# All of lookup level one on GpSimd, and the last layer-norm taken tile by tile on VectorE

## The chip, the cores and the metric

The kernel runs on one core of a Trainium2 chip. The core has four compute engines that run their own instruction streams in order and meet only at semaphores: TensorE (PE in the profile, its weight loads PEld), VectorE (DVE), ScalarE (ACT) and GpSimd (POOL). A fifth stream, SyncE (SP), issues all DMA transfers here. The metric is device microseconds from launch to end; lower is better. A profiled execution lists its own time, its span (first to last recorded instruction) and every instruction.

## What is computed

Two transformer layers over x of shape 4 x 256 x 256 (batch, sequence, width), each with attention, a sum and a layer-norm, a feed-forward part, a sum and a layer-norm:

```python
x = L0_attn_x                                        # (4, 256, 256)
x = layernorm(x + attn0(x))       # 32 query heads of 8, 8 key/value heads
x = layernorm(x + ffn0(x))        # weights rounded to fp8, scaled; inner width 768
x = layernorm(x + attn1(x))       # 16 query heads of 16, 8 key/value heads
x = layernorm(x + ffn1(x))        # w = lut[idx]: 16-entry table, int indices; inner width 688
# attn: softmax(q k^T / sqrt(d)) v, then the output projection
# ffn:  (silu(x @ gate) * (x @ up)) @ down
# layernorm(x) = (x - mean) / sqrt(var + 1e-5) over the width
```

## The kernel before

**Jobs.** There are eight jobs: 0 to 3 are layer 0 for batches 0 to 3, and 4 to 7 are layer 1 for the same batches. A job goes through these steps, whose names are used below. `q`, `kv`: projections on PE, split by ACT and POOL into three bf16 parts, which SP stacks into `QS` and `KS` (`qstack`, `kstack`). `max.j.u`: 4 matmuls into the PSUM tile `MM` and one VectorE reduce of 1024 columns to row maxima (16 units in a layer-0 job, 8 in a layer-1 job, 96 in all; there is one `MM`, so a unit's matmuls wait for the reduce before it). `mt`: the maxima are split, transposed, and put into `QS` by SP. `score`, `pv`: scores, exp on ACT (L838), probabilities times values. `turn`, `back`, `wo`: division, transposes and output projection, then `xadd` (POOL) and a layer-norm, whose statistics are VectorE's (L924, L929) and whose rest is POOL's (L653 to L657). `tr`: transpose of x. `gu.j.i`, `hsplit`, `down`: the feed-forward part in six row blocks; `down` of a job sums in one PSUM bank, ACT copies that out (L808), POOL adds it to x (`dsum`, L701), and the second layer-norm follows. `out`: the result's DMA, one per batch.

**Weights of the feed-forward parts.** Both are made on the core during the layer-0 jobs. Layer 0: 12 chunks (`q8`: ACT casts, a VectorE predicated copy at L1019, `q8w` on POOL). Layer 1: 10 chunks of 432 columns. For chunk c, `lutix` (ACT) makes bytes of the indices, `lutbits` (VectorE) picks out the four bits, and `lut1` computes eight table candidates from bit 0: `LV[:, i] = LT[2i] + bit * LD[i]`. Four of the eight are POOL's (L724, steps `lut1.c.0` and `lut1.c.1`) and four ACT's (L885, `lut1.c.2` and `lut1.c.3`), two instructions a step. `lut2`, `lut3`, `lut4` (VectorE, L1042) are predicated copies of 1728, 864 and 432 columns that leave one value; `lutlow` rounds it (ACT, L892) and takes the rest (POOL, L713), and SP writes that to DRAM. After chunk 9, ten `reload` transfers bring the low parts to SBUF over the space of `LV`. `lut1.c` waits for `lutlow` of chunk c - 1, and `lut2.c` waits for all eight candidates. The layer-1 feed-forward part cannot start before all of this.

**Order.** Nothing is scheduled at run time. `ORDER` holds one list of steps for each engine, written out by hand or by a program outside the kernel; each engine issues its list in order, and a step whose wait isn't met holds up everything behind it on that engine. An `@` in the list of PE names the one of three PSUM banks (`FB`) that the step takes.

Of the kernel before, what the change touches and what calls it, by code (L numbers as in the profile page):

```python
# [81 lines left out]
def unit0(j):  # L82
# [182 lines left out]
def two_layer_kernel(nc, x, xt, wq0, wk0, wv0, wo0, gate0, up0, down0, gs0, us0, ds0,  # L265
# [7 lines left out]
    with ExitStack() as ctx:  # L273
# [456 lines left out]
        def _(act):  # L730
            for step in order("ACT"):
# [144 lines left out]
                elif kind == "lut1":  # L876

                    _, c, part = step
                    if c == 0 and part == 2:
                        act.wait_ge(lut_steps, 1)  # L880
                    act.wait_ge(bit_done, c + 1)
                    if c >= 1:
                        act.wait_ge(low_done, c)
# [422 lines left out]
```

## Time and profile before

| | |
|---|---|
| runs | 363.84, 364.13, 361.82 us (median 363.84) |
| profiled execution | 362.06 us, of which the span 360.2 us |
| PE busy | 299.7 us (83%) |
| DVE busy | 258.1 us (72%) |
| ACT busy | 246.3 us (68%) |
| POOL busy | 195.2 us (54%) |
| `max` reduces, L950 | 96 of 1219 ns, 117.0 us |
| `lut1` on POOL, L724 | 40 of 715 ns, 28.1 us |
| `lut1` on ACT, L885 | 40 of 738 ns, 27.4 us |
| `lut2` to `lut4`, L1042 | 30 of 1419 ns, 42.6 us |

How to read it: the shares are averages over the whole span. The part up to about 200 us holds the four layer-0 jobs' attention and the making of the weights; the part behind it is mostly matmuls. Where a view gives "idle before <-X", the engine stood still until X was done.

### The profile page before, as it was taken

Reading aid. Unit: us, or ns where it says so; the run is one execution under the profiler, and the core shown is the slowest. Engines: PE = TensorE matmul, PEld = TensorE weight load, DVE = VectorE, ACT = ScalarE, POOL = GpSimd, SP = SyncE. Lnnn points to the kernel's source line nnn. Section 1 sums busy time; section 2 is a strip of 40 time slices with the busy share of each in tenths; the row PEclk is TensorE's granted clock in tenths of the full one; section 3 lists DMA queues with packets and bytes.
Section 4 is the critical chain, followed back from the end, with each engine's and each line's share of the span. In section 5 each row is a group of like instructions: output and inputs, shape, how many; then the busy total and the mean of one; then the engine's idle time right before and its main releaser. Section 6 shows DMA issues by size and latency. Waiting matters only on the chain.

```text
span 360.2 us, 7105 instructions
## 1 busy us (share of the span) xinstructions
PE 299.7 (83%) x2608; PEld 198.9 (55%) x2608; DVE 258.1 (72%) x399; ACT 246.3 (68%) x449; POOL 195.2 (54%) x261
## 2 busy tenths in 40 slices
PE   8446127687869897998979999999999999999990
PEld 7334002222426462564535765687778887979990
DVE  7695999898889897999986676656754657416341
ACT  3766677988588868797677776687677636654340
POOL 5756562404195348983398422564664346528763
PEclk9858555879899999999999999999999999999996
DMA  6468571201331000230001650032013000000000
GB/s 196 135 159 208 151 237 29 89 23 51 100 92 48 5 5 25 67 95 0 24 5 39 189 181 4 1 85 52 0 32 105 0 5 31 1 2 31 0 31 29
DMA packets 24872, 23.06 MB, mean 64 GB/s; under 512 B 3542, under 2 KB 24838, under 8 KB 24838
## 3 DMA queue, kind: packets, MB, share of 16 engines
q1 hardware_dynamic: 24838, 22.61, 22.2%
q8 instruction: 21, 0.34, 0.4%
q14 instruction: 13, 0.11, 0.1%
HBM read 10.47 MB, written 3.26 MB: 38 GB/s over the span
## 4 chain that ended last, share of the span: by engine, by line
PE 58%; DVE 13%; POOL 8%; ACT 8%; issue 7%; SPq 4%; DMA 2%; POOLq 0%; DVEq 0%; ACTq 0%
PE FB L1236 16%; PE PV L1179 9%; PE FB L1249 8%; PE MM L1124 6%; DVE LV L1042 5%; DVE MX L950 5%; PE SC L1158 4%; PE FB L1208 3%; PE SC L1153 2%; ACT PB L838 2%; PE FB L1078 2%; PE FB L1191 2%; SPq L542 2%; DMA QS<-QP 2%; ACT LV L885 2%
## 5 line engine op out<-in xcount | busy, mean ns | idle before, releaser
L950 DVE TENSOR_REDUCE MX<-MM 128x4 f32<-128x1024 f32 x96 | 117.0, 1219 | 40.1 <-PE MM L1124 39.5
L838 ACT ACTIVATE PB<-SC 128x1024 f32<-128x1024 f32 x96 | 98.2, 1023 | 31.7 <-PE SC L1153 19.5
L1124 PE MATMUL MM<-KS,QS 62*128 62x256 bf16 (+1 forms) x384 | 47.5, 292 | 33.6 <-DVE MX L950 24.8
L1179 PE MATMUL PV<-PB,VP 128*32 128x256 f32 x768 | 61.8, 408 | 1.3 <-ACT PB L838 1.3
L706 POOL TENSOR_TENSOR HL<-HF,HH 128x256 fp32r<-128x256 f32 (+1 forms) x48 | 37.6, 787 | 45.0 <-ACT HH L815 45.0
L1124 PEld LDWEIGHTS MM<-KS,QS 62*128 62x128 bf16 (+1 forms) x384 | 19.4, 97 | 59.4 <-DVE MX L950 39.4
L1042 DVE COPY_PREDICATED LV<-LB,LV 128x1728 f32<-128x1728 uint8 (+2 forms) x30 | 42.6, 1419 | 3.5 <-POOL LV L724 3.1
L1236 PE MATMUL FB<-XH,W 128*128 128x256 f32 x192 | 42.9, 305 | 0.5 <-DVE HF L1002 0.5
L1236 PE MATMUL FB<-XL,W 128*128 128x256 f32 x192 | 38.5, 282 | 0.0
L999 DVE SCALAR_TENSOR_TENSOR AA<-TH,FB 128x256 f32<-128x256 f32 (+1 forms) x48 | 20.0, 416 | 22.4 <-ACT TH L829 19.6
L1153 PE MATMUL SC<-QS,KS 64*128 64x256 bf16 x256 | 26.5, 287 | 9.8 <-ACT PB L838 7.8
L1236 PEld LDWEIGHTS FB<-XH,W 128*128 128x128 f32 x192 | 30.3, 190 | 6.5 <-issue 3.9
L1236 PEld LDWEIGHTS FB<-XL,W 128*128 128x128 f32 x192 | 29.5, 189 | 0.2 <-POOL XL L679 0.2
L1179 PEld LDWEIGHTS PV<-PB,VP 128*32 128x32 f32 x768 | 16.9, 110 | 22.6 <-issue 15.2
L724 POOL TENSOR_SCALAR LV<-LB,LD,LT 128x432 f32<-128x432 uint8 x40 | 28.1, 715 | 1.6 <-POOL LO L713 0.9
L885 ACT ACTIVATE LV<-LB,LT,LD 128x432 f32<-128x432 uint8 x40 | 27.4, 738 | 2.0 <-POOL LO L713 2.0
L657 POOL TENSOR_SCALAR X<-X,NM,RSTD 128x256 f32<-128x256 f32 x32 | 21.9, 693 | 1.7
L815 ACT ACTIVATE HH<-HF 128x256 fp32r<-128x256 f32 (+1 forms) x48 | 19.6, 412 | 4.6 <-DVE HF L1002 4.3
L1153 PEld LDWEIGHTS SC<-QS,KS 64*128 64x128 bf16 x256 | 8.9, 98 | 24.5 <-ACT PB L838 14.3
L1249 PE MATMUL FB<-W,HH 128*128 128x256 f32 (+1 forms) x96 | 22.0, 311 | 0.0
L664 POOL TENSOR_SCALAR W<-TH 128x384 fp32r<-128x384 f32 x12 | 6.9, 574 | 27.8 <-DVE TH L1019 27.8
L924 DVE BATCH_NORM_STATS2 BST<-X 128x6 f32<-128x256 f32 x32 | 11.9, 415 | 12.2 <-POOL X L701 11.9
(96 smaller groups left out, 578.5 us busy)
## 6 DMA issues: line engine op xcount, KB each, us to landing
QS<-QP SPq DMA_DIRECT2D x48, 128.0 KB, 2.4
IX<-in_idx SPq DMA_DIRECT2D x10, 216.0 KB, 4.0
dw<-LO SPq DMA_DIRECT2D x10, 216.0 KB, 2.1
W1L<-dw SPq DMA_DIRECT2D x10, 216.0 KB, 3.8
KS<-KP SPq DMA_DIRECT2D x24, 64.0 KB, 2.0
XT<-in_xt SPq DMA_DIRECT2D x4, 256.0 KB, 3.0
X<-in_x SPq DMA_DIRECT2D x4, 256.0 KB, 4.0
out<-X SPq DMA_DIRECT2D x4, 256.0 KB, 2.1
```

What stands on the lines that cost most here:

```text
L657: ins = pool.tensor_scalar(X[:, batch(j), t, :], X[:, batch(j), t, :], NM[:, n % 2, t:t + 1], RSTD[:, n % 2, t:t + 1], ALU.add, ALU.mult)
L706: pool.tensor_tensor(HL[0:r, i, :], HF[0:r, c % 2, :], HH[0:r, i, :].bitcast(F32), ALU.subtract).then_inc(h_parts, 1)
L724: ins = pool.tensor_scalar(LV[:, i, :], LB[:, 0, :], LD[:, i:i + 1], LT[:, 2 * i:2 * i + 1], ALU.mult, ALU.add)
L838: act.activation(PB[:, quad % PB_QUADS, kt, :, :], SC[:, :, :], ACT.Exp, scale=DH[layer(j)] ** -0.5).then_inc(exp_done, 1)
L885: ins = act.activation(LV[:, i, :], LB[:, 0, :], ACT.Identity, scale=LD[:, i:i + 1], bias=LT[:, 2 * i:2 * i + 1])
L950: dve.tensor_reduce(mx, MM[:, :, :].rearrange("p (f i) s -> p f i s", f=2), axis=AX.X, op=ALU.max).then_inc(max_red, 1)
L1042: ins = dve.copy_predicated(LV[:, 0:LUT // 2:2 * gap, :], mask, LV[:, gap:LUT // 2:2 * gap, :])
L1124: ins = pe.matmul(MM[:, 2 * f + i, :], QS[lo:lo + r, j % NST, qs + h, qt * P:(qt + 1) * P], keys(j)[lo:lo + r, j % NST, ks, :], start=True ...
L1153: ins = pe.matmul(SC[:, place(j, c), :], keys(j)[lo:lo + r, j % NST, ks, kt * P:(kt + 1) * P], QS[lo:lo + r, j % NST, qs + u % 4, :], star ...
L1179: ins = pe.matmul(PV[32 * c:32 * c + 32, r % 2, :], v, PB[:, quad % PB_QUADS, kt, place(j, c), :], start=part == 0, stop=part == (3, 1)[la ...
L1236: ins = pe.matmul(bank[:, w * S:(w + 1) * S], ffn_up(l, w, t, i)[part], xs[:, t, :], start=k == 0, stop=k == len(products) - 1)
L1249: ins = pe.matmul(bank[:, t * D:(t + 1) * D], hs[0:rows(l, i), i, t * P:(t + 1) * P], ffn_down(l, i)[part], start=i + k + t == 0, stop=(i, ...
```

## The change

Three things. `lut1` is four steps of POOL's list and none of ACT's; L742 of the new kernel is the POOL instruction that was L724 before, now 80 times. The last job's `down` goes to the two banks of `MM`, one row tile after the other; VectorE adds each tile to x straight from PSUM and takes its statistics and `var + eps`, POOL does one power per tile, VectorE the final subtract and multiply, and SP sends each tile by itself. All five lists are new.

```diff
 # waits of lut2 (VectorE)
-                        dve.wait_ge(level1, 2 * (c + 1))
-                        dve.wait_ge(level1_act, 2 * (c + 1))
+                        dve.wait_ge(level1, 4 * (c + 1))
 # ScalarE
-                elif kind == "lut1":
...
-                    for i in range(2 * part, 2 * part + 2):
-                        ins = act.activation(LV[:, i, :], LB[:, 0, :], ACT.Identity, scale=LD[:, i:i + 1],
-                                             bias=LT[:, 2 * i:2 * i + 1])
-                    ins.then_inc(level1_act, 1)
 # TensorE, down of the last job
+                    if j == JOBS - 1:
+                        if i == 0:
+                            pe.wait_ge(max_red, unit0(JOBS))
+                        for t in range(TT):
+                            for k, (part, hs) in enumerate(products):
+                                ins = pe.matmul(MM[:, 2 * t, :], hs[0:rows(l, i), i, t * P:(t + 1) * P],
+                                                ffn_down(l, i)[part], start=i + k == 0,
+                                                stop=(i, k) == (5, len(products) - 1))
+                            if i == 5:
+                                ins.then_inc(down_half, 1)
+                        continue
 # VectorE, down and fin of the last job
+                    for t in range(TT):
+                        dve.wait_ge(down_half, t + 1)
+                        link(dve.tensor_tensor(X[:, b, t, :], X[:, b, t, :], MM[:, 2 * t, :], ALU.add))
+                        link(dve.bn_stats(BST[:, n % 2, t, :], X[:, b, t, :]))
+                        link(dve.bn_aggr(MV[:, n % 2, t, :], BST[:, n % 2, t, :]))
+                        dve.tensor_scalar(VE[:, n % 2, t:t + 1], MV[:, n % 2, t, 1:2], 1.0, EPS, ALU.mult,
+                                          ALU.add).then_inc(var_last, 1)
+                elif kind == "fin":
...
+                    for t in range(TT):
+                        dve.wait_ge(rstd_last, t + 1)
+                        dve.tensor_scalar(X[:, b, t, :], X[:, b, t, :], MV[:, n % 2, t, 0:1], RSTD[:, n % 2, t:t + 1],
+                                          ALU.subtract, ALU.mult).then_inc(x_last, 1)
 # GpSimd, last job
+                            pool.wait_ge(var_last, t + 1)
+                            pool.tensor_tensor(RSTD[:, n % 2, t:t + 1], VE[:, n % 2, t:t + 1], NHALF[:, 0:1],
+                                               ALU.pow).then_inc(rstd_last, 1)
 # SyncE, last job
+                            sp.wait_ge(x_last, t + 1)
+                            sp.dma_start(out[batch(j), t * P:(t + 1) * P, :], X[:, batch(j), t, :]).then_inc(out_wr, 16)
 # the lists, one line of five tables
-        "q.0.0@0 q.0.1 kv.0.0@1 kv.0.1 kv.1.0@2 kv.1.1 q.1.0@0 q.1.1 max.0.0 q.2.0@1 q.2.1 q.3.0@0 q.3.1 max.0.1 "
+        "q.0.0@0 q.0.1 kv.0.0@1 kv.0.1 kv.1.0@2 kv.1.1 q.1.0@0 q.1.1 max.0.0 q.2.0@1 q.2.1 max.0.1 q.3.0@0 q.3.1 "
```

**Start of the program, PE.** Before, the second unit of maxima (`MM`) stands behind 8 matmuls of `q` for jobs 2 and 3 (two `FB` fills), and the third behind `kv.2`:

```order
L1124 MATMUL MM<-KS,QS 128x256 x4
L1078 MATMUL FB<-XT,WQ 128x256 x8
L1124 MATMUL MM<-KS,QS 128x256 x4
L1098 MATMUL FB<-XT,WK 64x256 x2
L1103 MATMUL FB<-WV,XT 128x64 x4
```

Now:

```order
L1150 MATMUL MM<-KS,QS 128x256 x4
L1104 MATMUL FB<-XT,WQ 128x256 x4
L1150 MATMUL MM<-KS,QS 128x256 x4
L1104 MATMUL FB<-XT,WQ 128x256 x4
L1124 MATMUL FB<-XT,WK 64x256 x2
L1150 MATMUL MM<-KS,QS 128x256 x4
L1129 MATMUL FB<-WV,XT 128x64 x4
```

The second unit moved ahead of `q.3`, the third ahead of half of `kv.2`.

**The same place, POOL.** Before, between the casts `q8w.0` (`W`) and the split of q of job 1 (`QR`), four candidates of chunk 0 (`LV`):

```order
L724 TENSOR_SCALAR LV<-LB,LD,LT 128x432 x2
L664 TENSOR_SCALAR W<-TH 128x384
L724 TENSOR_SCALAR LV<-LB,LD,LT 128x432 x2
L669 TENSOR_TENSOR QR<-QR,QP 128x512
L664 TENSOR_SCALAR W<-TH 128x384
```

Now eight, six of them ahead of that split and of `q8w.1`:

```order
L742 TENSOR_SCALAR LV<-LB,LD,LT 128x432 x2
L680 TENSOR_SCALAR W<-TH 128x384
L742 TENSOR_SCALAR LV<-LB,LD,LT 128x432 x6
L685 TENSOR_TENSOR QR<-QR,QP 128x512
L680 TENSOR_SCALAR W<-TH 128x384
```

Every chunk looks like this, with two to six candidates in a row. Chunk by chunk VectorE's `lut2` comes later in its list: `lut2.5`, behind `max.1.14` before, is now behind `max.2.4`; `lut2.7` went from behind `max.2.13` to behind `max.3.1`. For chunk 9 all three copies (`lut2.9`, `lut3.9`, `lut4.9`) stood ahead of `max.4.0` and now stand behind `gu.2.1`, `gu.2.5` and `max.4.5`. Up to `max.4.0` VectorE's new list lacks these three copies and is otherwise a reordering. PE's list up to `max.4.0` lacks `kv.5` and half of `q.5` (`q.5.1`) and has `score.3.7` and `pv.3.1.1` instead.

**The end, VectorE.** Before, the last rows (`AA` and `HF` are the last block of `gu`):

```order
L1002 SCALAR_TENSOR_TENSOR HF<-FB,AA 48x256
L924 BN_STATS BST<-X 128x6 x2
L929 BN_AGGR MV<-BST 128x2 x2
```

Now:

```order
L1029 SCALAR_TENSOR_TENSOR HF<-FB,AA 48x256
L1004 TENSOR_TENSOR X<-X,MM 128x256
L1005 BN_STATS BST<-X 128x6
L1006 BN_AGGR MV<-BST 128x2
L1007 TENSOR_SCALAR VE<-MV 128x1
L1004 TENSOR_TENSOR X<-X,MM 128x256
L1005 BN_STATS BST<-X 128x6
L1006 BN_AGGR MV<-BST 128x2
L1007 TENSOR_SCALAR VE<-MV 128x1
L1015 TENSOR_SCALAR X<-X,MV,RSTD 128x256 x2
```

The sum and the last multiply came over from POOL, and ACT's copy is gone.

## Rows read from the trace of the kernel before

**Rows 1.** Busy time per stretch; columns: length, then busy (x count) by engine.

```profile
30.00:60.00 30.00, 11.06 (x87) 3.89 (x86) 27.28 (x29) 21.18 (x44) 14.38 (x18) 0.60 0.55 163
60.00:100.00 40.00, 31.61 (x296) 12.02 (x288) 34.58 (x44) 33.12 (x57) 12.41 (x18) 0.83 0.21 62
100.00:200.00 100.00, 86.72 (x859) 49.59 (x856) 87.24 (x119) 79.29 (x133) 67.93 (x80) 1.00 0.14 39
200.00:347.00 147.00, 146.61 (x1265) 114.14 (x1265) 85.13 (x175) 93.08 (x176) 75.73 (x109) 1.00 0.15 44
```

**Rows 2.** Waits of PE from 0 to 200 us: total, times, longest.

```profile
PE MM L1124 <- DVE MX L950: 24.6, 23, 5.3
...
PE SC L1153 <- ACT PB L838: 7.8, 13, 0.9
```

**Rows 3.** Timeline of PE around the second unit: start, length.

```profile
23.45 6.61 PE L1078 MATMUL FB<-XT,WQ 128*128 128x256 f32 x16 [1.20 <-DMA XT<-in_xt]
29.99 0.39 PE L1124 MATMUL MM<-KS,QS 62*128 62x256 bf16 x4
```

**Rows 4.** Timeline of VectorE in the same stretch.

```profile
18.18 2.08 DVE L1042 COPY_PREDICATED LV<-LB,LV 128x1728 f32<-128x1728 uint8 x1 [3.12 <-POOL LV L724]
...
30.42 1.22 DVE L950 TENSOR_REDUCE MX<-MM 128x4 f32<-128x1024 f32 x1 [2.92 <-PE MM L1124]
```

**Rows 5.** The costliest groups: busy, mean ns, idle before.

```profile
L1042 DVE COPY_PREDICATED LV<-LB,LV 128x1728 f32<-128x1728 uint8 (+2 forms) x30 | 42.6, 1419 | 3.5 <-POOL LV L724 3.1
...
L999 DVE SCALAR_TENSOR_TENSOR AA<-TH,FB 128x256 f32<-128x256 f32 (+1 forms) x48 | 20.0, 416 | 22.4 <-ACT TH L829 19.6
...
L724 POOL TENSOR_SCALAR LV<-LB,LD,LT 128x432 f32<-128x432 uint8 x40 | 28.1, 715 | 1.6 <-POOL LO L713 0.9
L885 ACT ACTIVATE LV<-LB,LT,LD 128x432 f32<-128x432 uint8 x40 | 27.4, 738 | 2.0 <-POOL LO L713 2.0
```

**Rows 6.** Timeline of POOL at one `lut1`, of VectorE's `mt` beside it and alone.

```profile
48.45 2.76 POOL L724 TENSOR_SCALAR LV<-LB,LD,LT 128x432 f32<-128x432 uint8 x4
...
49.91 0.65 DVE L964 SCALAR_TENSOR_TENSOR MS<-MX,MS 128x32 bf16<-128x32 f32 x1
...
68.65 0.19 DVE L964 SCALAR_TENSOR_TENSOR MS<-MX,MS 128x32 bf16<-128x32 f32 x1
```

**Rows 7.** Timeline of VectorE: `lut2.9`, and the reduce of `max.4.0`.

```profile
187.81 2.10 DVE L1042 COPY_PREDICATED LV<-LB,LV 128x1728 f32<-128x1728 uint8 x1
...
197.34 1.23 DVE L950 TENSOR_REDUCE MX<-MM 128x4 f32<-128x1024 f32 x1 [2.35 <-PE MM L1124]
```

**Rows 8.** Timeline of PE: `kv.5` (two rows) and `q.5`.

```profile
189.89 1.13 PE L1098 MATMUL FB<-XT,WK 128*128 128x256 f32 x4
190.86 1.05 PE L1103 MATMUL FB<-WV,XT 128*128 128x128 f32 x8
...
194.36 2.00 PE L1078 MATMUL FB<-XT,WQ 128*128 128x256 f32 x8
```

**Rows 9.** Chain that ended last: start, length, what; its last matmuls.

```profile
347.56 4.47 PE FB L1249 x36
```

**Rows 10.** Timeline of all engines behind the last matmul.

```profile
352.06 0.60 ACT L808 ACTIVATE RAW<-FB 128x512 f32<-128x512 f32 x1 [2.55 <-PE FB L1249]
...
354.03 0.75 DVE L924 BATCH_NORM_STATS2 BST<-X 128x6 f32<-128x256 f32 x2 [4.97 <-POOL X L701]
354.82 0.25 DVE L929 BATCH_NORM_AGGREGATE MV<-BST 128x2 f32<-128x6 f32 x2
...
355.70 0.71 POOL L655 TENSOR_TENSOR RSTD<-VE,NHALF 128x2 f32<-128x2 f32 x1
356.51 1.10 POOL L657 TENSOR_SCALAR X<-X,NM,RSTD 128x256 f32<-128x256 f32 x2
...
357.64 0.37 SPq L610 DMA_DIRECT2D out<-X  x1
```

**Rows 11.** DMA issues of the output: KB each, median us to landing.

```profile
out<-X SPq DMA_DIRECT2D x4, 256.0 KB, 2.1
```

More of the change, by code:

```diff
@@ L412, in two_layer_kernel @@
         x_new = sem("x_new")
+        x_last = sem("x_last")
+        var_last = sem("var_last")
+        rstd_last = sem("rstd_last")
+        down_half = sem("down_half")
         th_done = sem("th_done")
@@ L429, in two_layer_kernel @@
         level1 = sem("level1")
-        level1_act = sem("level1_act")
         lut_done = sem("lut_done")
@@ L611, in _ @@
                                  X[:, batch(j), :, :]).then_inc(out_wr, 16)
-            sp.wait_ge(out_wr, 16 * B)
+            sp.wait_ge(out_wr, 16 * (B + TT - 1))
         @block.gpsimd
@@ L651, in _ @@
                     n = norms[step]
+                    if step == ("down", JOBS - 1):
+                        for t in range(TT):
+                            pool.wait_ge(var_last, t + 1)
+                            pool.tensor_tensor(RSTD[:, n % 2, t:t + 1], VE[:, n % 2, t:t + 1], NHALF[:, 0:1],
+                                               ALU.pow).then_inc(rstd_last, 1)
+                        continue
                     pool.wait_ge(mv_done, n + 1)
@@ L692, in _ @@
                     j = step[1]
+                    if j == JOBS - 1:
+                        continue
                     b = batch(j)
@@ L804, in _ @@
                     j = step[1]
+                    if j == JOBS - 1:
+                        continue
                     act.wait_ge(down_ready, j + 1)
@@ L875, in _ @@
                     act.activation(IB[:, :], IX[:, c % 2, :], ACT.Copy).then_inc(ib_done, 1)
-                elif kind == "lut1":
[L878 to L883, printed above, removed]
-                    for i in range(2 * part, 2 * part + 2):
-                        ins = act.activation(LV[:, i, :], LB[:, 0, :], ACT.Identity, scale=LD[:, i:i + 1],
-                                             bias=LT[:, 2 * i:2 * i + 1])
-                    ins.then_inc(level1_act, 1)
                 elif kind == "lutlow":
@@ L987, in _ @@
                     b = batch(j)
-                    dve.wait_ge(x_sum, j + 1)
-                    layer_norm(b, step)
+                    if j < JOBS - 1:
+                        dve.wait_ge(x_sum, j + 1)
+                        layer_norm(b, step)
+                        continue
+                    n = norms[step]
+                    dve.wait_ge(x_new, n - 1)
+                    for t in range(TT):
[6 more added lines that the diff above has]
+                elif kind == "fin":
+                    b = batch(JOBS - 1)
+                    n = norms["down", JOBS - 1]
+                    for t in range(TT):
+                        dve.wait_ge(rstd_last, t + 1)
+                        dve.tensor_scalar(X[:, b, t, :], X[:, b, t, :], MV[:, n % 2, t, 0:1], RSTD[:, n % 2, t:t + 1],
+                                          ALU.subtract, ALU.mult).then_inc(x_last, 1)
                 elif kind == "gu":
@@ L1246, in _ @@
                     products = ((0, HH), (0, HL), (1, HH))[:2 + l]
+                    if j == JOBS - 1:
+                        if i == 0:
+                            pe.wait_ge(max_red, unit0(JOBS))
+                        for t in range(TT):
+                            for k, (part, hs) in enumerate(products):
[4 more added lines that the diff above has]
+                                ins.then_inc(down_half, 1)
+                        continue
                     for k, (part, hs) in enumerate(products):
```

237 rows, old and new, of the table ORDER are left out of this document.

## Prediction, made before the changed kernel ran

> **What bounds the kernel now.** I read the stretches first [rows 1]. From 200 to 347 us PE is busy 146.6 of 147 us: nothing there can be gained except by giving PE less work or letting it begin earlier. From 30 to 200 us PE is not full: it is busy 11.1 of 30, 31.6 of 40 and 86.7 of 100 us. In the same three stretches VectorE is busy 27.3, 34.6 and 87.2 us, the highest or nearly the highest load of any engine. The waits of PE say the same [rows 2]: 24.6 us in 23 waits of a `max` unit for the reduce before it, and only 7.8 us in 13 waits of a `score` for ACT's exp. So up to about 200 us VectorE's list sets the pace, with PE's list order deciding how well it is fed; behind that PE does. The crossing is the reduce of `max.4.0` at 197.34 us [rows 7]. The kernel ends with a serial tail: the last matmul ends just before ACT's copy at 352.06 us, and copy, sum, statistics, power, multiply and one transfer follow, each waiting for the one before it [rows 10, 11].
>
> Hence the questions: does the new order bring `max.4.0` sooner, how much PE work stands behind it, and what is left of the tail. All sums are against the profiled execution (362.06 us).
>
> **The tail.** Before, from 352.06 to the end of POOL's multiply at 356.51 + 1.10 = 357.61 us: 5.55 us, then the transfer [rows 10]. After, PE finishes row tile 0 three matmuls before the end. The 36 matmuls of `down` take 4.47 us [rows 9], 0.124 us each, so 0.37 us early, at about 351.7 us. Per tile VectorE then has an add from PSUM, 0.42 us like the 256-column form of L999 [rows 5], half of 0.75 us of statistics, half of 0.25 us of aggregation and a one-column operation of 0.1 us [rows 10]: 1.0 us, and with three own-semaphore waits of about 0.1 us each 1.3 us. Two tiles: 351.7 + 2.6 = 354.3 us. The power of tile 1 costs 0.71 us plus a crossing of 0.1 us, 355.1 us; the last subtract and multiply 0.35 to 0.55 us (POOL took 0.55 for a tile), 355.5 us. Against 357.61 us this is 2.1 us less; the transfer is half as large, but its 2.1 us to landing [rows 11] is kept since four transfers of one size don't show how it depends on size. Ends: 1.3 us if every link costs 0.2 us and the multiply 0.55, 2.8 us if the half transfer lands sooner. **-2.1 us.**
>
> **The start.** The second unit of maxima waits in PE's list behind 6.61 us of projections [rows 3], and VectorE stands still 2.92 us before its reduce at 30.42 us [rows 4]. The new list puts only half of those projections ahead of it: it can begin about 3.3 us sooner. Against this stands `lut1.0`: eight candidates on POOL cost 8 x 0.715 = 5.7 us instead of 2.9 us on each of two engines [rows 5], so `lut2.0`, which began at 18.18 us as soon as POOL was done [rows 4], begins 2.8 us later, and the first reduces queue behind it. Part of that is free, since VectorE has the 2.9 us hole behind it and the next cast is put ahead. Walking the new list by these durations brings the first `mt` about 3.3 us sooner with 0.8 us of copies fewer ahead of it. I take **-2.0 us**, ends 0 and -3.3.
>
> **Chunk 9 goes behind the crossing.** VectorE's list up to `max.4.0` lacks `lut2.9`, `lut3.9`, `lut4.9`. Ten chunks are 42.6 us [rows 5], with stalls in it; the first copy of chunk 9 took 2.10 us [rows 7] and the other two are a half and a quarter of its columns, together 3.9 us. They land where VectorE is busy 85 of 147 us [rows 1], and `reload` still has some 40 us until job 4's feed-forward part. Cover gone, that is if a unit of maxima had to wait for them there, they would cost up to the same 3.9 us again. **-3.9 us**, ends 0 and -4.3.
>
> **More PE work behind the crossing.** `kv.5` is 1.13 + 1.05 us and half of `q.5` is 1.0 us [rows 8], less overlap of 0.2: 3.0 us that are now behind `max.4.0`. Ahead of it instead are a `score` of four matmuls, priced as the four of a `max` (0.39 us, [rows 3]), and a `pv` part, again four matmuls of 256 columns, 0.4 to 0.65 us. As PE is full from there on, the difference counts: **+2.0 us**, ends +1 and +2.5.
>
> **`lut1` alone on POOL.** In sum POOL gets 28.6 us, and from 100 to 200 us, where five of the ten chunks lie, it goes from 67.9 busy to about 82 of 100 us [rows 1]. POOL does not become full, but `lut2.c` now waits 2.8 us more for its candidates, and behind it on VectorE stand units of maxima and behind these PE. The new list gives room for this: between `lutbits.c` and `lut2.c` VectorE has mostly four to six units of maxima, six to nine us. POOL's list between them holds 5.7 us of candidates and, for chunk 5, a layer-norm of some 2.8 us too (8.5 against 7.6 us), for chunk 7 the layer-norm of `down.0` ahead and one `hsplit` between. I price two or three late chunks at 0.5 to 1 us: **+1.5 us**, ends 0 and +6.
>
> **Port contention.** While POOL ran `lut1`, VectorE's small `mt` operation took 0.65 us, against 0.19 us with POOL still [rows 6]. `lut1.c` cannot meet the copies of its own chunk, since they wait for it; it can meet the 12 casts' predicated copies, `mt` and `lutbits`. Some 40 such operations, a sixth of them beside a new `lut1`, at up to 0.46 us each is 3 us at the most, and part of it in VectorE's idle time. **+1.0 us**, ends 0 and +3. The Trainium skill (SBUF — State Buffer, "Who interferes with whom") calls the shared port pair of VectorE and GpSimd an exclusive lock, held for a whole instruction, so that the loser "fully blocks". By that rule an operation that starts in a random place in a 0.71 us instruction loses 0.36 us on the mean, and the forty would add 2.4 us instead of 1.0; the trace's 0.46 us agrees with it.
>
> **ACT relieved.** It loses 40 x 0.738 us = 29.5 us of instructions (27.4 us busy, as they overlap) [rows 5]. ACT was busy 33.1 of 40 us from 60 to 100 us and 79.3 of 100 behind that [rows 1], but PE waited for exp only 7.8 us [rows 2], and much of that hides under the next reduce. **-1.0 us**, ends 0 and -5.
>
> **Sum.** -2.1 - 2.0 - 3.9 + 2.0 + 1.5 + 1.0 - 1.0 = -4.5 us: 357.6 us on the scale of the profiled execution. That execution lies 1.8 us below the median of the runs; on the median's scale it is 359.3. I put the forecast between them, at **358.5 us**.
>
> **The rivals.** (a) *Only the tail counts.* The lists trade places without gain: what the start and chunk 9 save goes into the later `kv.5`, later copies and waits for `lut2`. For it: the terms of the lists sum to only -2.4 us, and in-order lists lose easily what they gain. Against it: the 2.92 us hole and chunk 9's copies are real and their new places are free. 363 (between the profiled execution and the median) - 2.1 gives 361 us. Chance 0.27. (b) *Slower: the candidates come late in nearly every chunk.* The place is VectorE's wait at `lut2.c`; each chunk late by the 2.8 us that POOL's extra four candidates take costs up to 10 x 2.8 = 28 us, of which the room in the list takes most. It decides against the change where the mean lateness is above 0.6 us (6.0 us with the 1.5 already counted cancel the gain), and at 1.4 us, half of the extra, the time is 358.5 + 14 - 1.5 = 371 us. For it: VectorE's list is served in order and is the bound there, POOL is at 82%, and POOL's durations stretch where it meets VectorE's copies. Against it: six to nine us of room. Chance 0.10. (c) *ACT was the hidden limit.* With ACT free, exp follows its score at once and `mt`, `stage` and casts come sooner; the 7.8 us of waits mostly go and the start gives its full 3.3 us: 358.5 - 4 - 1.3 = about 353.5 us. For it: ACT's 83% from 60 to 100 us. Against it: these waits are short (0.9 us at most). Chance 0.18. (d) *The tail does not do what it says:* the four linked operations per tile cost as much as the shorter chain saves. 360.5 us; it would need 0.4 us more per link. Chance 0.03. My forecast keeps 0.42.
>
> **Range and chances.** 353 us leaves out the better half of what is beyond (c), 363 us takes in (a) and (d) whole; (b) lies outside. About 1% either way is what a measurement of this kernel can tell from no change: faster means under 360.2 us, slower above 367.5 us. Faster: my forecast nearly whole (0.39), (c) (0.18) and a little of (a) and (d) (0.05), 0.62. Slower: (b) without its mild end, 0.09. Same: 0.29.
>
> **What would show it.** In the new profile: the second reduce of `MX` at about 27 us instead of 30.4; `max.4.0` (the 65th of 96 reduces) at 191 to 194 us instead of 197.3; no wait of VectorE's copies for POOL over 1 us behind the first chunk; PE full from there on; from the last matmul to the last multiply 3.5 us instead of 5.6, and two transfers in the place of one. Wrong would be: waits of L1068 for L742 of several us in total (rival b); `max.4.0` sooner but the last matmul not (PE's later work or new waits behind 200 us took it); or PE's waits for exp gone and the crossing below 190 us (rival c).

## The result, and the profile after

The changed kernel takes **358.64 us** (median, 357.35 to 358.93) beside 363.05 us (361.82 to 364.13) for the kernel before on the same chip: ratio 0.988, interval 0.9855 to 0.991. The forecast was 358.5 us, inside 353 to 363. The sum came out; several of its terms did not, as the experiments show, so part of the hit is luck.

The profiled execution of the changed kernel took 358.93 us, 357.0 us of it span. First the stretches, with the columns of [rows 1]:

```profile
30.00:60.00 30.00, 12.41 (x91) 4.51 (x94) 27.57 (x30) 15.83 (x34) 23.99 (x30) 0.58 0.57 160
60.00:100.00 40.00, 30.50 (x328) 11.46 (x320) 36.32 (x45) 32.86 (x55) 20.89 (x27) 0.97 0.23 64
100.00:200.00 100.00, 85.61 (x824) 48.88 (x826) 88.34 (x119) 66.05 (x107) 73.92 (x97) 0.98 0.12 35
200.00:347.00 147.00, 146.55 (x1258) 114.23 (x1255) 88.11 (x177) 94.88 (x180) 79.74 (x114) 1.00 0.16 46
```

PE is as full from 200 us on as before. ACT lost 13 us between 100 and 200 us, POOL gained 6 us there. The column behind the five engines is the clock granted to TensorE, as a share of the higher of its two levels (1.00 is 2.4 GHz, 0.50 is 1.2 GHz, values between are a mixture in time). From 60 to 100 us it is 0.97, where it was 0.83 [rows 1]. No run changes the clock by itself, so what this is worth stays open; PE's busy time for its 2608 matmuls is 298.9 us beside 299.7, which leaves little for it.

VectorE was to get no new work but the short tail, and yet is busier in every stretch. The page says where (the busy line, then three of the costliest groups):

```profile
PE 298.9 (84%) x2608; PEld 197.6 (55%) x2608; DVE 267.7 (75%) x405; ACT 224.6 (63%) x408; POOL 222.9 (62%) x297
...
L958 DVE TENSOR_REDUCE MX<-MM 128x4 f32<-128x1024 f32 x96 | 117.1, 1220 | 34.9 <-PE MM L1150 34.1
...
L742 POOL TENSOR_SCALAR LV<-LB,LD,LT 128x432 f32<-128x432 uint8 x80 | 56.3, 716 | 0.9 <-DVE LB L1054 0.6
...
L1068 DVE COPY_PREDICATED LV<-LB,LV 128x1728 f32<-128x1728 uint8 (+2 forms) x30 | 45.9, 1531 | 3.0 <-POOL LV L742 2.8
```

VectorE's total went from 258.1 to 267.7 us; 1.9 us of the growth are the six instructions that the new tail adds. The thirty copies have the same count as in [rows 5], and their mean went from 1419 to 1531 ns. They wait for POOL 2.8 us in all, nearly all of it at the first chunk (3.1 us before): candidates that come late are not the matter.

The start, on VectorE, answers to [rows 4], and the maxima's crossing to [rows 7]:

```profile
22.23 3.04 DVE L1068 COPY_PREDICATED LV<-LB,LV 128x1728 f32<-128x1728 uint8 x1 [2.63 <-POOL LV L742]
25.31 1.23 DVE L958 TENSOR_REDUCE MX<-MM 128x4 f32<-128x1024 f32 x1
...
28.60 1.21 DVE L958 TENSOR_REDUCE MX<-MM 128x4 f32<-128x1024 f32 x1
...
192.20 1.22 DVE L958 TENSOR_REDUCE MX<-MM 128x4 f32<-128x1024 f32 x1 [1.88 <-PE MM L1150]
193.46 0.51 DVE L970 TENSOR_SCALAR MS<-MX 128x32 bf16<-128x32 f32 x1
194.00 0.65 DVE L972 SCALAR_TENSOR_TENSOR MS<-MX,MS 128x32 bf16<-128x32 f32 x1
194.64 1.23 DVE L958 TENSOR_REDUCE MX<-MM 128x4 f32<-128x1024 f32 x1
197.62 1.23 DVE L958 TENSOR_REDUCE MX<-MM 128x4 f32<-128x1024 f32 x1 [1.76 <-PE MM L1150]
```

The first reduce is 3.0 us later than before (22.28 us), the second 1.8 us sooner, and the unit of `max.4.0` begins at 194.64 instead of 197.34 us. The starts of a few steps on VectorE, read from the timelines in list order, show when the new order is ahead (for a unit of maxima the start of its reduce; the last two columns are experiments described below):

| start of, us | before | after | tail alone | lists and POOL alone |
|---|---|---|---|---|
| `max.0.0` | 22.28 | 25.31 | 21.97 | 24.58 |
| `mt.0.0` | 49.40 | 48.96 | 48.94 | 48.38 |
| `mt.0.1` | 68.44 | 65.30 | 67.98 | 64.76 |
| `max.2.0` | 110.03 | 103.05 | 109.31 | 102.84 |
| `mt.2.1` | 153.97 | 149.75 | 153.25 | 150.29 |
| `mt.3.1` | 194.25 | 193.46 | 193.55 | 193.25 |
| `max.4.0` | 197.34 | 194.64 | 196.63 | 194.43 |
| `max.5.0` | 221.40 | 220.15 | 220.68 | 219.95 |
| `lut2.5` | 105.28 | 114.24 | 104.54 | 114.03 |
| `lut2.9` | 187.81 | 201.97 | 187.11 | 201.77 |
| end of the last matmul | 352.03 | 351.44 | 351.25 | 351.33 |

The lead is 7.0 us at `max.2.0`. In part that is because the copies of each chunk from the sixth on come some 9 to 14 us later, and the lead shrinks as they follow. At `mt.3.1` 0.8 us are left and at the last matmul 0.6 us.

The tail, all engines from the last matmul on, answers to [rows 10]; the last row is the page's kind for the output, to be read against [rows 11]:

```profile
351.16 0.28 PE L1279 MATMUL MM<-W1L,HH 48*128 48x256 f32 x1
351.19 0.42 DVE L1004 TENSOR_TENSOR X<-X,MM 128x256 f32<-128x256 f32 x1 [2.71 <-PE MM L1279]
...
352.40 0.41 DVE L1004 TENSOR_TENSOR X<-X,MM 128x256 f32<-128x256 f32 x1
...
353.60 0.40 DVE L1015 TENSOR_SCALAR X<-X,MV,RSTD 128x256 f32<-128x256 f32 x1
353.76 0.65 POOL L665 TENSOR_TENSOR RSTD<-VE,NHALF 128x1 f32<-128x1 f32 x1 [0.64 <-DVE VE L1007]
354.03 1.20 SPq L616 DMA_DIRECT2D out<-X  x2
354.44 0.41 DVE L1015 TENSOR_SCALAR X<-X,MV,RSTD 128x256 f32<-128x256 f32 x1 [0.45 <-POOL RSTD L665]
```

```profile
out<-X SPq DMA_DIRECT2D x2, 128.0 KB, 1.7
```

From the end of the last matmul (351.44) to the end of the last multiply (354.85) it is 3.4 us instead of 5.55, and a half transfer lands in 1.7 us instead of 2.1.

### The profile page after: what moved, and what is told of

Same layout as the page of the kernel before. It is cut to its first block, busy times and chain, and to the rows that moved or that the text cites. A ratio compares the mean times of both kernels' runs of the same rounds, so it can differ in the third digit from the quotient of the medians.

```text
span 357.0 us, 7099 instructions
## 1 busy us (share of the span) xinstructions
PE 298.9 (84%) x2608; PEld 197.6 (55%) x2608; DVE 267.7 (75%) x405; ACT 224.6 (63%) x408; POOL 222.9 (62%) x297
## 4 chain that ended last, share of the span: by engine, by line
PE 55%; DVE 16%; POOL 9%; ACT 6%; issue 6%; SPq 5%; DMA 2%; POOLq 0%; ACTq 0%; DVEq 0%
PE FB L1262 14%; PE PV L1205 9%; PE FB L1287 7%; DVE LV L1068 6%; PE MM L1150 5%; DVE MX L958 5%; PE SC L1184 4%; PE FB L1234 4%; POOL LV L742 4%; ACT PB L858 3%; PE SC L1179 3%; PE FB L1217 2%; SPq L546 2%; POOL LO L731 2%; PE FB L1243 2%
## 5 line engine op out<-in xcount | busy, mean ns | idle before, releaser
L1150 PE MATMUL MM<-KS,QS 62*128 62x256 bf16 (+1 forms) x384 | 47.6, 293 | 35.4 <-DVE MX L958 27.3
L1205 PE MATMUL PV<-PB,VP 128*32 128x256 f32 x768 | 60.4, 400 | 2.9 <-ACT PB L858 2.6
L724 POOL TENSOR_TENSOR HL<-HF,HH 128x256 fp32r<-128x256 f32 (+1 forms) x48 | 37.1, 777 | 32.2 <-ACT HH L835 32.1
L742 POOL TENSOR_SCALAR LV<-LB,LD,LT 128x432 f32<-128x432 uint8 x80 | 56.3, 716 | 0.9 <-DVE LB L1054 0.6
L1068 DVE COPY_PREDICATED LV<-LB,LV 128x1728 f32<-128x1728 uint8 (+2 forms) x30 | 45.9, 1531 | 3.0 <-POOL LV L742 2.8
L731 POOL TENSOR_TENSOR LO<-LV,W 128x432 f32<-128x432 f32 x10 | 11.5, 1145 | 21.7 <-ACT W L900 21.6
L706 POOL TENSOR_TENSOR X<-X,WF 128x512 f32<-128x512 f32 x8 | 11.2, 1395 | 16.5 <-ACT WF L820 16.5
L1104 PE MATMUL FB<-XT,WQ 128*128 128x256 f32 x64 | 18.8, 440 | 1.2 <-DMA XT<-in_xt 1.2
L1184 PE MATMUL SC<-QS,KS 98*128 98x512 bf16 x64 | 19.2, 382 | 0.4 <-ACT PB L858 0.4
L1287 PE MATMUL FB<-W,HH 128*128 128x256 f32 (+1 forms) x84 | 19.1, 309 | 0.2 <-POOL HL L724 0.2
```

Source lines behind the costliest of these rows:

```text
L724: pool.tensor_tensor(HL[0:r, i, :], HF[0:r, c % 2, :], HH[0:r, i, :].bitcast(F32), ALU.subtract).then_inc(h_parts, 1)
L742: ins = pool.tensor_scalar(LV[:, i, :], LB[:, 0, :], LD[:, i:i + 1], LT[:, 2 * i:2 * i + 1], ALU.mult, ALU.add)
L1068: ins = dve.copy_predicated(LV[:, 0:LUT // 2:2 * gap, :], mask, LV[:, gap:LUT // 2:2 * gap, :])
L1150: ins = pe.matmul(MM[:, 2 * f + i, :], QS[lo:lo + r, j % NST, qs + h, qt * P:(qt + 1) * P], keys(j)[lo:lo + r, j % NST, ks, :], start=True ...
L1184: ins = pe.matmul(SC[:, 2 * f:2 * f + 2, :], keys(j)[lo:lo + r, j % NST, ks, kt * P:(kt + 1) * P], QS[lo:lo + r, j % NST, qs:qs + 2, :], s ...
L1205: ins = pe.matmul(PV[32 * c:32 * c + 32, r % 2, :], v, PB[:, quad % PB_QUADS, kt, place(j, c), :], start=part == 0, stop=part == (3, 1)[la ...
```

## The experiments

All twelve were timed in five rounds beside the kernel before, with four to twelve runs each. "Ratio" is to that kernel in the same rounds, with its 95% interval. The median of the kernel before moved between 361.72 and 363.05 us from one set of rounds to another, so kernels of different sets are compared by their ratios.

**Taking the change apart.** `t1_tail`: the kernel before, its lists and its shared level one, with the new tail. `t2_lists`: the new lists and all of level one on GpSimd, with the old tail.

> The kernel before with the new tail only: its five lists and ScalarE's half of level one stay, the last job's sums go tile by tile on VectorE from the two maxima banks. By the two traces, the time from the last matmul to the end of the span went from 352.03 -> 360.2 us (8.2 us) to 351.44 -> 357.0 us (5.6 us), so this kernel should be 2.6 us faster than before (about 360.4 us against 363.05 us); my forecast's own term was 2.1 us. Rival: the tail gains only because the new lists leave VectorE and GpSimd idle there; then it is under 1 us faster. Last matmul in the trace: unmoved at about 352 us by both.

> The five new lists and GpSimd alone on level one, with the old tail (copy by ScalarE, sum and layer-norm by GpSimd, one transfer). Theory A: the lists move the last matmul by only 0.6 us (352.03 to 351.44 us in the traces), because what chunk 9's deferral and the start gain is lost to the port shared by VectorE and GpSimd and to the projections put off; this kernel is then 0.5 to 2 us faster than before (361 to 362.5 us). Rival: the lists carry most of the whole 4.4 us gain, which the single traces understate; then it is 3 us or more faster (under 360 us).

The tail alone: 359.76 us, ratio 0.9939 (0.9915 to 0.9962), 2.2 us. The lists and GpSimd alone: 361.31 us, ratio 0.9974 (0.9955 to 0.9992), 0.9 us. Together 3.2 us by the ratios, and the whole change measured 0.988, which is 4.3 us: they add up within the intervals. The tail is between half (2.2 of 4.3) and two thirds (2.2 of 3.2) of the gain.

The profiled executions do not show the rest. Set beside the tail alone, the changed kernel has its first reduce 3.3 us later, then needs 5.3 us less from there to `max.4.0`, and 2.2 us more from `max.4.0` to the end of the last matmul (156.80 against 154.62 us), which ends 0.2 us later. The profiled execution of `t1_tail` took 358.60 us, near the lowest of its twelve runs (358.46 to 361.55), so a gain of 1 to 2 us is seen only in the ratios.

**Everything on GpSimd under the old lists** (`t4_pool`), and **the new lists with ACT sharing again** (`t3_share`: four of the eight candidates go back to ACT, at places in its list that I chose by the times in the trace).

```diff
 t4_pool, list of GpSimd, every chunk
-lut1.c.0 .. lut1.c.1
+lut1.c.0 .. lut1.c.1 lut1.c.2 lut1.c.3
```

> The kernel before, lists and tail as they were, but each chunk's four ScalarE candidates stand behind GpSimd's four. Nothing in the lists gives room for them. Theory A: VectorE's copies wait 1 to 2.8 us more in many of the ten chunks and its operations grow beside GpSimd's longer runs, the end is 3 to 9 us later, 366 to 372 us. Rival B: ScalarE's relief pays for it, 361 to 363.5 us.

> The changed kernel, but ScalarE takes four of the eight candidates of every chunk again (put into its list where the chunk's bits and the low part of the chunk before are done by the changed kernel's trace; GpSimd's list without them, all else the same). Theory A (the shared port eats the gain): VectorE's busy time falls by 4 to 8 us (its operations beside long runs of GpSimd instructions shrink), and the end comes 1 to 3 us earlier than in the changed kernel, 356 to 357.5 us. Rival B (ScalarE's relief is what pays): exp waits behind the candidates again, and it is 1 to 3 us slower than the changed kernel, 360 to 362 us. No difference would mean that neither matters behind the crossing to the TensorE-bound part.

`t4_pool`: 387.64 us, ratio 1.0697 (1.0652 to 1.0743). VectorE's waits over the whole span (us in total, times, longest):

```profile
DVE MX L921 <- PE MM L1094: 43.7, 40, 2.9
...
DVE LV L1012 <- POOL LV L707: 15.6, 6, 4.7
```

and two of PE's:

```profile
PE FB L1187 <- POOL X L640: 11.8, 4, 4.4
...
PE SC L1123 <- ACT PB L821: 5.1, 10, 0.9
```

This is rival (b) in the flesh: up to 4.7 us of waiting for candidates, six times, and the layer-norms behind them late too (PE waits 11.8 us for x from GpSimd, 1.7 us before). The waits seem to cost twice, since the granted clock fell behind them: from 115 to 120 us PE was busy 1.28 of 5 us while it waited for such a layer-norm, and from 120 to 125 us it was granted 0.50, the lower level. Over 100 to 150 us the clock is 0.85 instead of 1.00, and PE's 2608 matmuls are busy 309.6 us instead of 299.7. The new lists are the condition of the change.

`t3_share`: 377.67 us, ratio 1.0444 (1.0405 to 1.0483). Its VectorE is busy 257.0 us instead of 267.7, but it waits 55.6 us in 53 waits for maxima from PE and PE 16.2 us for exp, and PE is busy 311.8 us instead of 298.9, at a granted clock of 0.84 instead of 0.97 from 100 to 150 us. My places for ACT's steps were bad. VectorE's total is 10.7 us lower without GpSimd's extra candidates, but in a kernel whose engines meet at other times; the run says nothing on which split is faster.

**The start.** `s1_start` puts the second unit ahead of `q.3` in the kernel with the new tail; `a1_start` undoes just that in the changed kernel.

```diff
 s1_start, list of PE (a1_start: the reverse)
-max.0.0 q.2.0 q.2.1 q.3.0 q.3.1 max.0.1
+max.0.0 q.2.0 q.2.1 max.0.1 q.3.0 q.3.1
```

> The kernel before with the new tail (measured alone at 0.994) and one more edit: on the tensor engine the second maximum's products stand ahead of the fourth query projection. Forecast's term for the start: the second reduce begins at about 28 us instead of 30, and 1.5 to 2.5 us of it last to the end, because the vector engine binds the first 190 us: about 358, ratio 0.988. Rival, from the milestones of the changed kernel: a lead gained at the start is spent when the tensor engine becomes the bound at about 190 us, so the time stays that of the new tail alone, 359.8, ratio 0.994, although the second reduce comes 2 us earlier.

> The changed kernel with the one edit at the start undone: on the tensor engine the second maximum's products stand behind the fourth query projection again. If the start's term of 2 us lasts to the end: 360.5, ratio 0.993 against the kernel before. If it is spent at the crossing to the tensor engine's bound: 358.6 to 359, ratio 0.988, although the second reduce comes 2 to 3 us later.

`s1_start`: 360.12 us, ratio 0.9931 (0.9902 to 0.996), the same as the tail alone. `a1_start`: 358.80 us, ratio 0.9908 (0.9877 to 0.9939), overlapping that of the changed kernel; it is 0.2 us from it by the median and 0.9 us by the ratios. So this one move is worth nothing that can be measured here. A gain of under 1 us would be missed, and the rest of the new start (the third unit, the earlier cast) was not tried by itself. VectorE's reduces in `t1_tail`, and then in `s1_start`:

```profile
29.77 1.23 DVE L955 TENSOR_REDUCE MX<-MM 128x4 f32<-128x1024 f32 x1 [2.65 <-PE MM L1148]
32.13 1.23 DVE L955 TENSOR_REDUCE MX<-MM 128x4 f32<-128x1024 f32 x1 [1.14 <-PE MM L1148]
...
47.69 1.23 DVE L955 TENSOR_REDUCE MX<-MM 128x4 f32<-128x1024 f32 x1 [0.71 <-PE MM L1148]
```

```profile
27.38 1.23 DVE L955 TENSOR_REDUCE MX<-MM 128x4 f32<-128x1024 f32 x1 [0.20 <-PE MM L1148]
32.36 1.23 DVE L955 TENSOR_REDUCE MX<-MM 128x4 f32<-128x1024 f32 x1 [3.75 <-PE MM L1148]
...
47.71 1.23 DVE L955 TENSOR_REDUCE MX<-MM 128x4 f32<-128x1024 f32 x1 [0.71 <-PE MM L1148]
```

The second reduce is 2.4 us sooner, the third 0.2 us later: 2.65 + 1.14 us of waiting became 0.20 + 3.75. The projection of `q.3` did not go away, it only stands in front of the next unit, and PE was the bound in this stretch. I had read a hole of VectorE as its own to fill.

My second theory was that such a lead is kept until about 190 us and spent when PE becomes the bound. For the start it fell with the same rows: the lead is gone at 32 us.

**Chunk 9 alone.** `s2_late9` is `s1_start` with chunk 9's copies behind `max.4.1`, `max.4.2` and `max.4.3`, and its later steps on ACT, GpSimd and SP moved back to match.

```diff
 s2_late9, list of VectorE (wo.2 down to gu.2.1)
-max.3.13 lut2.9 max.3.14 lut3.9 max.3.15 lut4.9 mt.3.1 max.4.0 gu.2.0 max.4.1 gu.2.1
+max.3.13 max.3.14 max.3.15 mt.3.1 max.4.0 gu.2.0 max.4.1 lut2.9 gu.2.1
```

> As the run with the early second maximum, and the nine copies of lookup chunk 9 stand behind maxima of the fifth job's first tiles instead of ahead of its first one (the scalar engine still takes half of level one). Forecast's term: max.4.0 begins 3.9 us earlier and the end comes 3.9 us earlier, about 355 if the start's term holds too, ratio 0.978. Rival: the copies are only deferred and the tensor engine is the bound from there on, so max.4.0 comes 3 to 4 us earlier but the end at most 1 us: 358 to 360, ratio 0.988 to 0.994.

361.65 us, ratio 0.9973 (0.995 to 0.9995): 1.5 us *slower* than `s1_start` by the medians, which neither side had. The intervals of the two ratios overlap a little, but the traces agree: `s2_late9` starts the reduce of `max.4.0` at 195.81 us, 0.9 us ahead of `s1_start`, and that of `max.5.0` at 222.39, 1.65 us behind it, and its last matmul ends 1.63 us later. VectorE in `s1_start` before `mt.3.1`, then in `s2_late9`, and then PE's next wait in `s2_late9`:

```profile
187.16 2.10 DVE L1066 COPY_PREDICATED LV<-LB,LV 128x1728 f32<-128x1728 uint8 x1
189.29 1.23 DVE L955 TENSOR_REDUCE MX<-MM 128x4 f32<-128x1024 f32 x1
190.43 1.13 DVE L1066 COPY_PREDICATED LV<-LB,LV 128x864 f32<-128x864 uint8 x1
191.91 1.23 DVE L955 TENSOR_REDUCE MX<-MM 128x4 f32<-128x1024 f32 x1 [0.35 <-PE MM L1148]
```

```profile
188.35 1.23 DVE L955 TENSOR_REDUCE MX<-MM 128x4 f32<-128x1024 f32 x1 [1.16 <-PE MM L1148]
191.80 1.23 DVE L955 TENSOR_REDUCE MX<-MM 128x4 f32<-128x1024 f32 x1 [2.22 <-PE MM L1148]
...
201.60 2.10 DVE L1066 COPY_PREDICATED LV<-LB,LV 128x1728 f32<-128x1728 uint8 x1
```

```profile
204.72 0.66 PE L1215 MATMUL FB<-IDN,ST 128*128 128x128 f32 x4 [1.48 <-DVE HF L1026]
```

With the copies gone VectorE merely waits 1.16 + 2.22 us for PE, and the reduce at 191.80 is 0.1 us sooner. The copies had lain in time in which PE was already the bound, and in their new place the first stands ahead of a `gu` that PE needs: 1.48 us of PE's time at a place where it is otherwise full.

**ACT relieved and nothing else.** `t5_actfree` is the kernel before without ACT's level one steps from the second chunk on; half of the candidates are old values there.

> The kernel before, in which the scalar engine makes its half of the level one candidates for the first chunk only; for the nine others its steps are left out, and levels two to four select among old values. That is the relief of the scalar engine by itself, some 27 us of its work, with nothing added on GpSimd. Forecast: 1.0 us, 362; rival (a) nothing; rival (c), a hidden limit on the scalar engine: 5 us or more, 358 or less. If this gain is large, the changed kernel must have lost most of it elsewhere.

362.21 us, ratio 0.9998 (0.998 to 1.0017). ACT is busy 225.5 us instead of 246.3, and it buys nothing under the old lists. In the changed kernel PE's waits for exp (`SC` and `PV` for `PB`) are 9.3 us up to 200 us, 8.9 before. Rival (c) is out as it was told, with those waits gone; whether a free ACT helps under the new lists was not tried by itself.

**GpSimd relieved in the changed kernel.** `a2_half` leaves out half of the candidates from the second chunk on.

```diff
 a2_half, GpSimd's lut1
+                    if c >= 1 and part >= 2:
+                        continue
```

> The changed kernel, in which GpSimd makes candidates 0 to 3 of all chunks but candidates 4 to 7 of the first chunk only; for the nine others those steps are left out and the copies select among old values. It takes 27 us of work off GpSimd and gives it to no engine. Forecast: candidates that come late and the shared port cost 1.5 + 1.0 us together, so the time falls to about 356.1, ratio 0.981. If the port's cost on the path is as large as the 8 us by which VectorE's busy time grew: 351 or less. Rival, from the runs so far: the 8 us lie in slack that the tensor engine's bound leaves, so VectorE's busy time falls by 5 us or more and the time by less than 1: 358 to 358.6, ratio 0.988.

356.12 us, ratio 0.982 (0.9787 to 0.9854), so 2.5 us less than the changed kernel by the medians and 2.3 us, 0.6%, by the ratios, whose intervals (0.9855 is the lower end of the changed kernel's) meet end to end, with four runs on each side. VectorE's total is 261.0 us instead of 267.7. Its groups by shape (busy, mean ns, then idle before), first of the changed kernel, then of `a2_half`:

```profile
L1068 DVE COPY_PREDICATED LV<-LB,LV 128x1728 f32<-128x1728 uint8 x10 | 26.3, 2626 | 2.9 <-POOL LV L742 2.8
...
L1054 DVE TENSOR_TENSOR LB<-IB,BITS 128x432 int32<-128x432 int32 x10 | 10.1, 1011 | 0.0
```

```profile
L1070 DVE COPY_PREDICATED LV<-LB,LV 128x1728 f32<-128x1728 uint8 x10 | 22.8, 2281 | 2.6 <-POOL LV L744 2.6
...
L1056 DVE TENSOR_TENSOR LB<-IB,BITS 128x432 int32<-128x432 int32 x10 | 8.1, 805 | 0.0
```

The waits for candidates differ by 0.2 us, so late candidates are not what the 2.5 us are. PE's waits for reduces up to 200 us fall from 27.3 to 23.7 us, and its waits for GpSimd's x hardly at all (0.6 to 0.4 us), which points to VectorE's instructions being longer beside GpSimd's. That they are all of it is argued, not shown, and the size of the growth is partly chance: `a1_start`, which has all the candidates and is as slow as the changed kernel, has a VectorE total of 262.6 us, with the large copies at 2400 ns. So the candidates lengthen VectorE's work by 1.6 to 6.7 us from trace to trace, and the time does not follow that total one to one.

The lead of `a2_half` over the changed kernel is 1.0 us at `max.1.0`, 2.0 at `max.2.0`, 2.8 at `mt.2.0` and still 2.8 at `max.7.0`. Of this 0.8 us stand already at the first reduce (24.52 against 25.31), before any candidate is left out; beside `t2_lists`, whose first reduce is at 24.58, the lead is 2.6 us at `mt.2.0` and at `max.7.0`. What is saved before about 130 us is kept.

**What on GpSimd does it.** Both kernels are the one before, with work added behind each of GpSimd's twenty `lut1` steps (only the added instructions are shown, without their waits).

```diff
 t7_read
+  pool.tensor_scalar(SCR[:, n, :], <432 columns that are read>, ..)      # twice a step
 t8_write
+  pool.memset(SCR[:, n, :], 0.0)                                         # three times a step, 373 columns
```

> The kernel before, and behind each of GpSimd's twenty level one steps two more tensor_scalar instructions of 432 columns that read and write on-chip memory into a scratch area (1.4 us each step, 27 us in all). The scalar engine keeps its half, the lists are untouched. If a GpSimd instruction of this kind holds up VectorE's copies for as long as it runs: VectorE's busy time grows by some us, on the copies of 1728 columns and the threshold instructions above all. If it takes only GpSimd's time: VectorE's groups keep their means, and only waits for POOL grow. Time: 364 to 368 by either.

> As the run with the extra tensor_scalars, but with three memsets of 373 columns instead (about 1.2 us a step by the fill's own length): they write on-chip memory and read nothing. If a GpSimd instruction holds VectorE up whatever it does, VectorE's copies are as long as with the tensor_scalars; if only operands that are read do it, they keep the means of the kernel before. Time: 363 to 368.

`t7_read`: 382.64 us, ratio 1.0567 (1.0524 to 1.061). `t8_write`: 373.41 us, ratio 1.03 (1.0268 to 1.0332). Both far above what I expected: the extra work also made the candidates late (8.5 and 4.9 us of VectorE's waits), and the times can't tell the cause. The means by shape say a little: the large copy goes from 2200 ns before to 2316 with the tensor_scalars and 2161 with the memsets; the threshold instruction of 96 columns (`BIG`, 268 ns before) to 494 and 439. VectorE, then GpSimd in `t8_write`:

```profile
18.98 2.08 DVE L1050 COPY_PREDICATED LV<-LB,LV 128x1728 f32<-128x1728 uint8 x1 [4.17 <-POOL LV L726]
...
33.48 1.15 DVE L1023 TENSOR_SCALAR BIG<-AA 128x96 int32<-128x96 int32 x1
```

```profile
18.90 1.10 POOL L734 MEMSET SCR<- 128x373 f32 x3
20.12 1.92 POOL L671 TENSOR_TENSOR QR<-QR,QP 128x512 f32<-128x512 f32 x1
...
33.46 1.10 POOL L734 MEMSET SCR<- 128x373 f32 x3
```

The large copy beside three memsets takes its undisturbed 2.08 us. The threshold instruction, 0.20 us when alone, lasts until the memsets end at 34.56. This is one case of each. The means agree, but one copy of 3.5 us in place of one of 2.1 moves the mean of ten by 0.14 us, about as much as separates these kernels. Why the two kinds differ stays open.

**A version stretched further.** `s3_spread` is the changed kernel with chunk 7 in chunk 8's place, chunk 8 in chunk 9's, and chunk 9 at 222 us and later, on all queues.

> The changed kernel with the lookup stretched further: chunk 7 stands where chunk 8 stood (behind the fourth job's tenth tile), chunk 8 where chunk 9 stood, and chunk 9 behind the sixth job's tiles at 222 to 236 us, on all five queues; the reload follows at about 240, and the first product that reads it stands at 273. If VectorE still binds up to 170 us, the tensor engine's 2.8 us of waits for freed maxima banks between 140 and 170 shrink and the end comes 1 to 2 us earlier: 357, ratio 0.984. Rival: another partner (the scalar engine's exponentials) takes the waits over, and the late copies cost what they did in the run with chunk 9 late, 1.5 us: 358.6 to 360.

372.27 us, ratio 1.0273 (1.0241 to 1.0304). At `max.5.0` it is ahead of the changed kernel by 1.1 us (219.06 against 220.15), the size that was expected, but 0.7 us of that stand already at the first reduce (24.63 against 25.31), where the lists are the same. Then my new chunk 9 breaks it on VectorE:

```profile
226.36 2.07 DVE L1051 COPY_PREDICATED LV<-LB,LV 128x1728 f32<-128x1728 uint8 x1 [3.53 <-POOL LV L725]
...
235.27 1.23 DVE L941 TENSOR_REDUCE MX<-MM 128x4 f32<-128x1024 f32 x1 [4.85 <-PE MM L1133]
```

The copy waits 3.5 us for its candidates, the `turn` queued behind it is late, PE waits 5.2 us for that (`FB` for `NT`), and at `max.6.0` the kernel is 7.6 us behind. The version is worthless, and whether a lead of this size is real or could be kept was not tried. No run with the whole computation beat the changed kernel.

## Why the prediction was right, step by step

- **Tail, -2.1 us: right**, with the mechanism and the size (2.2 us alone; 3.4 us from last matmul to last multiply, forecast 3.5). The transfer, kept at its old price, gave 0.4 us more.
- **Start, -2.0 us: wrong, about 0 for the move that was tried.** The failed step is "walking the new list by these durations", which was to bring the first `mt` 3.3 us sooner; it came 0.4 us sooner (48.96 against 49.40). It counted the projection that was moved behind the unit as gone. VectorE's gap moved to the next reduce (`s1_start`), and undoing the edit in the changed kernel cost 0.2 us. The first reduce was 3.0 us late, as the eight candidates said.
- **Chunk 9, -3.9 us: wrong as a term for that chunk.** The step "VectorE's list sets the pace up to `max.4.0`" failed: PE took over before, the 2.35 us before `max.4.0` in [rows 7] said so, and I read them as the crossing itself. Chunk 9 lay in slack: moving it alone brought `max.4.0` 0.9 us sooner instead of 3.9, and cost 1.5 us at the end.
- **More PE work behind the crossing, +2.0 us: the size is there, its cost is not tested.** From the start of the reduce of `max.4.0` to the end of the last matmul it is 154.69 us before and 156.80 us after, 2.1 us more. But if PE is the bound on both sides of `max.4.0`, it matters little which side the work stands on, and the term is about 0; that is argued only.
- **`lut1` alone on POOL, +1.5 us of waits: the lists give the room.** Waits of the copies for POOL are 0.2 us in all behind the first chunk. Under the old lists they are 15.6 us and the time of the whole kernel 7% longer.
- **Port contention, +1.0 us: mechanism right, size too small.** VectorE's time grew by 9.6 us: 1.9 are the tail's own instructions, and 1.6 to 6.7, by the trace, hang on the four extra candidates, which cost 2.5 us at the end. The step that failed is "`lut1.c` can only meet casts, `mt` and `lutbits`": it left out that the copies meet all the other work of GpSimd, which now stands packed behind `lut1`. The two terms together were +2.5 us, and `a2_half` gives 2.5 us, by luck in the split.
- **ACT relieved, -1.0 us: 0 under the old lists** (0.9998). The 7.8 us that `score` waited for exp were 6.7 us afterwards, but `pv` waited 2.6 us for it instead of 1.1, with 13 us less on ACT from 100 to 200 us.
- **What the lists gave.** `a2_half` less its tail (0.982 against 0.9939) leaves 1.2%, 4.3 us, for the lists with ACT free and GpSimd as loaded as before; ACT free gave nothing under the old lists, and the start nothing here. What is left is the other moves, likely the copies from the sixth chunk on that leave the stretch up to about 130 us, where VectorE does bind. The table of starts agrees up to `max.2.0`, but no run moved them alone, and the profiled executions show none of it at the last matmul, so this cause stays open. The higher granted clock from 60 to 100 us is a rival that no run sets apart. Split this way the account is: tail -2.2, lists -4.3, candidates +2.3, together -4.2 us. It adds up by construction, since the last two terms are differences to the same run; the one independent sum, tail and `t2_lists`, gives -3.2. The forecast had -2.1, -4.9 (start, chunk 9, PE's later work, ACT) and +2.5.
- **So the number was right in part by luck.** The tail was understood. The -4.9 us for the lists was a sum of a start and a chunk 9 that gave nothing, ACT that gave nothing, and a loss that may not be one; by this split a gain of about that size came from somewhere that the forecast did not name.
- **Rivals.** (a) foresaw 361 us, a ratio of 0.994, which the interval of the change excludes; its picture (the lists give little net) was half right, 0.9 us by `t2_lists`. (b) is real and was held off by the lists. (c) is out as it was told, (d) is out.

## What to carry to other kernels

A gap of one engine in front of an item is no gain to be had by moving that item forward, unless the engine that feeds it is idle too: look at the next two items, the gap may only move there. Which engine binds is told by who waits for whom in each short stretch; here it changed before the busy shares did. Work that lies where its engine waits for another costs nothing there, and moving it away can hurt, as it did with chunk 9. A profiled execution is one run: compare its first milestones before reading a lead of 1 us out of later ones. When work is handed to GpSimd, price it twice: its own time, and the growth of VectorE's instructions wherever the two run together.

## What the hardware showed that I had not expected

An instruction of VectorE that meets GpSimd can wait through *several* instructions in a row. VectorE, then GpSimd in the changed kernel:

```profile
155.41 4.44 DVE L1068 COPY_PREDICATED LV<-LB,LV 128x1728 f32<-128x1728 uint8 x1
```

```profile
155.34 1.41 POOL L724 TENSOR_TENSOR HL<-HF,HH 128x256 fp32r<-128x256 f32 x2
156.70 1.16 POOL L685 TENSOR_TENSOR QR<-QR,QP 128x512 f32<-128x512 f32 x1
158.09 2.25 POOL L690 TENSOR_TENSOR KR<-KR,KP 128x256 f32<-128x256 f32 x1 [0.23 <-ACT KR L781]
```

Alone such a copy takes 2.10 us [rows 7]. Here it ends at 159.85, so it ran from about 157.8, when GpSimd's third instruction ended, and waited 2.3 us. Then GpSimd waits in turn: its next one, 0.67 us at other places, lasts 2.25 us, to 0.5 us behind the copy's end. In `t2_lists` the same copy took 4.14 us. A threshold instruction of 96 columns took 2.04 us beside three instructions of GpSimd without a gap (30.43 to 32.82 us), and 0.20 us alone:

```profile
30.86 2.04 DVE L1042 TENSOR_SCALAR BIG<-AA 128x96 int32<-128x96 int32 x1
```

It is not always so. In `a1_start`, with the same two lists, GpSimd's pair `HL` began at 155.81 us and the copy at 156.53, about when the first of the pair was done. The copy took 2.09 us, and the pair 3.36 us instead of 1.41. So which of the two waits hangs on small differences in time, and VectorE's total changes by some us from trace to trace. That a queue of GpSimd packed without gaps costs VectorE more than the same instructions with gaps is likely from these rows, but no run varied the gaps alone.

The Trainium skill (SBUF — State Buffer, "Who interferes with whom") says that the loser of the shared port waits for a whole instruction. The trace agrees that the loser waits, here 2.3 us, and the 4.44 us row goes beyond a single instruction: three. The 2.09 us of `a1_start` show that this does not happen at every meeting.
